# Edge stages of a graph-network kernel: ScalarE's loop announces its closing branch with a prefetch hint

## The chip, the core and the metric

The kernel runs on one NeuronCore of one Trainium2 chip. The metric is the device time of one execution in microseconds (us). Five engines run their own instruction streams and meet through semaphores: TensorE (PE, with its weight loads as PEld), VectorE (DVE), ScalarE (ACT), GpSimd (POOL) and the sync engine (SP), which issues DMAs.

## The reference, cut to what matters

The reference works on 6,250 nodes with 128 features and 100,000 edges sorted by destination. It chains two attention blocks over the graph. The first block has two GATv2 layers, and these are the edge stages that the change is about:

```python
def _gatv2(x, edge_index, Wl, bl, Wr, br, att, bias):
    ...
    xl = (x @ Wl + bl).reshape(n, h, d)
    xr = (x @ Wr + br).reshape(n, h, d)
    e = jax.nn.leaky_relu(xl[src] + xr[dst], NEG_SLOPE)
    score = jnp.einsum('ehd,hd->eh', e, att)
    m = jax.ops.segment_max(score, dst, num_segments=n)
    ex = jnp.exp(score - m[dst])
    denom = jax.ops.segment_sum(ex, dst, num_segments=n)
    alpha = ex / denom[dst]
    out = jax.ops.segment_sum(alpha[:, :, None] * xl[src], dst, num_segments=n)
    return out.reshape(n, h * d) + bias
...
x_in = _gatv2(x, edge_index, Wl1, bl1, Wr1, br1, att1, bc1)
h = jax.nn.relu(_batchnorm(x_in @ W1 + b1, g1, be1))
h2 = _gatv2(h, edge_index, Wl2, bl2, Wr2, br2, att2, bc2)
```

Each layer has three heads of 128 features. A third, different attention over the same edges (`edge_attention`) follows and is not touched.

## The kernel before

The kernel first sorts the edges, then runs GAT layer 1, a node layer, GAT layer 2, a second node layer, and the last attention. Both GAT layers call the same function, `gat_edges`, which is written once and so stands twice in every engine's program.

In `gat_edges` the edges and self loops are cut into 464 groups of 2 tiles of 128. Per group POOL gathers rows of the `xl` table into a ring in `feat_area` (L1332), PE looks up the destination's rows with one-hot matrices (L1382), DVE adds the two (L1524) and applies the leaky relu and the attention weights (L1532), and ScalarE sums each row over the features to a score (`reduce`, L1474: an ACTIVATE and an ACTIVATION_READ_ACCUMULATOR per tile and head, six pairs a group). Every eighth group closes a chunk: the scores are copied out (L1480), turned, scanned for the maximum of each destination and exponentiated (L1450, L1451). Eleven groups behind `reduce`, ScalarE multiplies the gathered rows by their weights (`weight`, L1458, four or six ACTIVATEs a group), and PE sums the weighted rows by destination (L1395) into `node_area`.

The order on each engine is written by `pipeline`. It takes stages with leads, writes the first groups out, then a loop whose turn holds `unroll` groups, then the last groups. In the edge stages `unroll` is 16. Each engine has its own loop with its own counter, so nothing joins the engines at the end of a turn but the semaphores of the stages. ScalarE's call is L1482. For it the loop runs over turns 2 to 28, which is 27 turns and 26 jumps back in each layer. Of ScalarE's program before, as it is built, a turn is 313 instructions of 64 bytes, the closing branch included. The loop's first instruction is number 1145 of that program in layer 1 and number 2110 in layer 2, counted from 0 without labels.

In the text below "loop 1" and "loop 2" are ScalarE's loops of `gat_edges` in layers 1 and 2, and a "turn" is one pass through such a loop. Operations that belong to the loop itself (counter, branch, the registers set at its head) have line L125.

Of the kernel before, what the change touches and what calls it, by code (L numbers as in the profile page):

```python
# [84 lines left out]
def later(g, n=1):  # L85

    return not isinstance(g, int) or g >= n
# [7 lines left out]
def snapped(eng, value):  # L95

    return value if isinstance(value, int) else eng.snap(value)


def pipeline(eng, groups, stages, unroll=2, number=False):  # L100

    ahead, behind = max(lead for lead, _ in stages), min(lead for lead, _ in stages)

    def at(turn, s):
        numbers = {}
        for lead, fn in stages:  # L110
            q = s + lead
            if isinstance(turn, int) and not 0 <= unroll * turn + q < groups:
                continue
            if not number:
                fn(turn + q // unroll, q % unroll)
                continue
            if q not in numbers:
                numbers[q] = snapped(eng, unroll * turn + q)
            fn(turn + q // unroll, q % unroll, numbers[q])

    first = -(-(unroll - behind) // unroll)
    last = (groups - ahead) // unroll
    for t in range(-ahead, unroll * first):
        at(t // unroll, t % unroll)
    with eng.Fori(first, last) as i:  # L125
        for s in range(unroll):
            at(i, s)
    for t in range(unroll * last, groups - behind):
        at(t // unroll, t % unroll)
# [135 lines left out]
def sort_by_dst(k, io, beside):  # L265
# [196 lines left out]
    with nc.Block() as block:  # L462
        @block.sync
        def _(sp):
            def load_keys(j, s):
                if s % 2:
                    return
                h = R * j + s
                if reused(j):
                    sp.wait_ge(ohT_ready, h - R + 2)  # L470
                sp.dma_start(lo_bc[s // 2], k.lo_edge[ds(h * (HALF * P), 2 * HALF * P)].partition_broadcast(P)
                             ).then_inc(bc_ready[s // 2], 16)

            pipeline(sp, halves, [(0, load_keys)], R)
            beside.on_sync(sp)
            src_moves.store(sp, k.moved_s, beside.moved_i)
            sp.sem_inc(sorted_src, 1)
            norm_on_sync(sp)
            table_on_sync(sp)

        @block.scalar
        def _(act):
# [15 lines left out]
            def mark_earlier(j, s):  # L498
# [4 lines left out]
                nc.scalar.activation(earlier[s % 2], match[s % 2], ACT.Relu).then_inc(earlier_set, 1)  # L503

            pipeline(act, halves, [(1, round_table), (1, keep_rows), (1, mark_earlier)], R)
            dst_moves.on_scalar(act)
            beside.on_scalar(act, multiplied, halves)
# [6 lines left out]
        def _(pe):  # L514
# [42 lines left out]
            def count_earlier(j, s):  # L557
# [5 lines left out]
                last.then_inc(looked, 1)  # L563

            pipeline(pe, halves, [(1, flip_keys), (1, match_keys), (0, update), (0, look_up), (0, count_earlier)], R)
            dst_moves.on_tensor(pe)
            beside.on_tensor(pe, dst_moves)
# [707 lines left out]
def gat_edges(k, att, tag, late):  # L1275

    nc = k.nc
    groups, U = GROUPS, 2 * CG
# [16 lines left out]
    first = [cut(1) for _ in range(2)]  # L1295
# [22 lines left out]
    def chunk(j, s):  # L1318
        return 2 * j + s // CG

    with nc.Block() as block:
        @block.gpsimd
        def _(pool):
            for g in range(groups):
                s = g % U
                if g >= U:
                    pool.wait_ge(summed, g - U + 1)
                    pool.nop(nofuse=True)
                for u in range(GS):
                    at = s * W + u * HE  # L1330
                    rows = k.gather_col[:, g * GS + u:g * GS + u + 1]
                    pool.indirect_dma_start(ring[:, at:at + HE], None, k.xl,  # L1332
                                            bass.IndirectOffsetOnAxis(ap=rows, axis=0)).then_inc(gathered[s], 16)
                late.write(pool, (g + 1) * LATE_GAT // groups - g * LATE_GAT // groups)
# [105 lines left out]
        @block.scalar  # L1440
        def _(act):
            def exps(j, s):
                if s % CG != CG - 1:
                    return
                c = chunk(j, s)
                act.wait_ge(shifted, c + 1)
                act.wait_ge(dropped, c + 1)
                if later(c):
                    act.wait_ge(back, c)
                nc.scalar.activation(ex, shift, ACT.Exp)  # L1450
                nc.scalar.activation(fade, drop, ACT.Exp).then_inc(exped, 1)  # L1451

            def weight(j, s):
                act.wait_ge(weights, chunk(j, s) + 1)
                for u in range(GS):
                    for h in range(H - 1 if s % 4 == 0 else H):
                        row = ring4[:, s * GS + u, h, :]
                        last = nc.scalar.activation(row[:, 0:D], row[:, 0:D], ACT.Copy, scale=row[:, D:D + 1])  # L1458
                last.then_inc(weighted, 1)

            def reduce(j, s):
                g = U * j + s
                c = chunk(j, s)
                act.wait_ge(weighed, g + 1)
                if s % CG == 0:
                    if later(c, 2):
                        act.wait_ge(scored, c - 1)
                    else:
                        act.wait_ge(preset, 1)
                for u in range(GS):  # L1470
                    for h in range(H):
                        at = z[s % V][:, u * HE + h * DW:u * HE + (h + 1) * DW]
                        to = h * CROW + s % CG * GS + u
                        last = nc.scalar.activation(at, at, ACT.Copy, accum_out=score_in[s // CG][:, to:to + 1])  # L1474
                last.then_inc(reduced, 1)
                if s % CG == CG - 1:
                    act.wait_ge(reduced, g + 1)
                    if later(c, 2):
                        act.wait_ge(turned, c - 1)
                    nc.scalar.copy(score[s // CG], score_in[s // CG]).then_inc(scored, 1)  # L1480

            pipeline(act, groups, [(-3, exps), (-11, weight), (0, reduce)], U)  # L1482

        @block.vector
        def _(dve):
# [792 lines left out]
```

## Time and profile before

| what | value |
|---|---|
| time, median of 3 runs | 6345.56 us |
| lowest and highest of the 3 | 6339.74, 6350.01 us |
| the profiled execution's own time | 6317.56 us |
| its span in the trace, first to last instruction | 6315.4 us |
| ACT busy over the span | 4432.6 us, 70% |
| DVE busy over the span | 5297.8 us, 84% |

The profiled execution took 28 us less than the median of the timed runs. Busy shares over the whole span mix stages with different limits, so the profile has to be read loop by loop: which engine has hardly any idle time in the stretch, what ended its idle time, and what the same program text did in the other layer. "Idle before, releaser" tells what an instruction waited for. "issue" there means that the trace shows no semaphore or transfer that ended the wait. The queue q14 of the DMA list is of the kind "instruction": it brings engines their own program.

### The profile page before, as it was taken

How to read it: one execution, taken by the hardware profiler on the slowest of the kernel's cores; microseconds unless marked ns; L12 is line 12 of the kernel's file. 1: busy time of each engine (PE TensorE's matmuls, PEld its weight loads, DVE VectorE, ACT ScalarE, POOL GpSimd, SP SyncE). 2: the span in 40 equal slices, each digit the busy share in tenths (PEclk: the TensorE clock that was granted, in tenths of full speed). 3: DMA queues.
4: the chain of work that ended last, by engine and by line, in shares of the span. 5: the costliest groups of instructions: out<-in, count | busy, mean ns of one | idle time of the engine just before them, and what ended most of it. 6: DMA issues, size and time to landing. Idle time of an engine off the chain costs nothing. (4 is left out here: it accounts for less than half of the span.)

```text
span 6315.4 us, 122309 instructions
## 1 busy us (share of the span) xinstructions
PE 4846.5 (77%) x22358; PEld 2873.2 (45%) x22359; DVE 5297.8 (84%) x12463; ACT 4432.6 (70%) x19858; POOL 4274.3 (68%) x3722
## 2 busy tenths in 40 slices
PE   3799689558988888888788888888888766666563
PEld 2575345234444444444644444444444445555552
DVE  9998898659999999999678898988888766666666
ACT  6487679429999999999278888888888553333332
POOL 0488777837777777776576676666666557777773
PEclk9999999779999999999899999999999977777776
DMA  0243000235555555556154444544445234444444
GB/s 16 54 86 30 2 2 2 31 116 144 140 139 140 137 141 139 140 139 114 27 152 130 125 129 127 131 124 127 129 125 124 42 106 130 128 129 128 129 129 77
DMA packets 342152, 657.19 MB, mean 104 GB/s; under 512 B 99030, under 2 KB 190100, under 8 KB 341506
## 3 DMA queue, kind: packets, MB, share of 16 engines
q0 software_dynamic: 191520, 481.83, 30.7%
q1 hardware_dynamic: 150370, 172.99, 10.7%
q14 instruction: 234, 1.92, 0.1%
q8 instruction: 28, 0.46, 0.0%
HBM read 618.58 MB, written 34.84 MB: 103 GB/s over the span
## 5 line engine op out<-in xcount | busy, mean ns | idle before, releaser
L1332 POOL DMA_INDIRECT feat_area<-xl_table,gather_col x1856 | 2178.9, 1174 | 948.3 <-issue 531.1
L1382 PE MATMUL bank<-node_area,feat_area 128*128 x3712 | 1481.2, 523 | 331.9 <-DVE feat_area L1524 146.2
L1458 ACT ACTIVATE feat_area<-feat_area 128x128 f32<-128x128 f32 x5104 | 1608.6, 419 | 145.8 <-issue 145.8
L1474 ACT ACTIVATE feat_area<-feat_area 128x130 f32<-128x130 f32 x5568 | 1500.4, 331 | 256.2 <-DVE feat_area L1532 254.4
L1395 PE MATMUL bank<-feat_area 128*128 128x390 f32 x3712 | 1433.4, 509 | 138.6 <-ACT feat_area L1458 90.2
L1382 PEld LDWEIGHTS bank<-node_area,feat_area 128*128 128x128 f32 x3712 | 646.9, 193 | 954.1 <-issue 701.7
L1474 ACT ACTIVATION_READ_ACCUMULATOR feat_area<-feat_area 128x1 f32 x5568 | 1054.3, 190 | 0.0
L1395 PEld LDWEIGHTS bank<-feat_area 128*128 128x128 f32 x3712 | 694.6, 195 | 694.8 <-issue 293.8
L2020 POOL DMA_INDIRECT feat_area<-kv_table,gather_src x832 | 808.1, 971 | 280.6 <-issue 252.1
L1524 DVE TENSOR_TENSOR feat_area<-bank,feat_area 128x780 f32<-128x780 f32 x928 | 890.0, 959 | 62.4 <-DMA feat_area<-xl_table,gather_col 43.8
L650 POOL DMA_INDIRECT word_by_dst<-feat_area,gather_col x640 | 791.8, 1237 | 195.0 <-issue 188.9
L1532 DVE SCALAR_TENSOR_TENSOR feat_area<-feat_area 128x780 f32<-128x780 f32 x928 | 889.8, 959 | 0.0
L2060 PE MATMUL bank<-feat_area 128*128 128x136 f32 x1664 | 362.1, 382 | 424.5 <-DVE feat_area L2131 423.7
L675 POOL DMA_INDIRECT word_by_src<-lo_src,gather_src x336 | 441.5, 1314 | 301.3 <-issue 146.4
L2073 ACT ACTIVATE feat_area<-feat_area 128x32 f32<-128x32 f32 x208 | 47.7, 229 | 734.5 <-DVE feat_area L2120 734.5
L2060 PEld LDWEIGHTS bank<-feat_area 128*128 128x128 f32 x1664 | 306.0, 267 | 473.6 <-DVE node_area L2146 326.7
L1571 DVE SCALAR_TENSOR_TENSOR node_area<-node_area,stays,bank 128x390 f32 x812 | 496.8, 612 | 15.5 <-PE bank L1395 15.3
L901 PE MATMUL bank<-feat_area 125*128 125x416 f16 (+1 forms) x2496 | 460.5, 347 | 7.9 <-ACT feat_area L917 4.8
L917 ACT ACTIVATE feat_area<-feat_area 125x128 f16<-125x128 f16 x1248 | 399.2, 390 | 75.2 <-DVE feat_area L875 64.2
L2107 DVE TENSOR_TENSOR feat_area<-feat_area,bank 128x512 f32<-128x512 f32 x208 | 143.1, 688 | 288.8 <-DMA feat_area<-kv_table,gather_src 284.2
L1063 DVE TENSOR_TENSOR feat_area<-iota_f,lo_col 128x256 f32<-128x256 f32 x928 | 384.6, 414 | 0.0
L901 PEld LDWEIGHTS bank<-feat_area 125*128 125x128 f16 x2496 | 243.6, 98 | 224.8 <-DVE feat_area L877 9.2
(363 smaller groups left out, 7140.4 us busy)
## 6 DMA issues: line engine op xcount, KB each, us to landing
feat_area<-lo_slot SPq DMA_DIRECT2D x464, 128.0 KB, 3.3
feat_area<-xl_table,gather_col POOLq DMA_INDIRECT x1856, 3.5
feat_area<-lo_slot_src SPq DMA_DIRECT2D x104, 256.0 KB, 3.4
node_area<-lo_edge SPq DMA_DIRECT2D x100, 256.0 KB
xl_table<-feat_area SPq DMA_DIRECT2D x98, 195.0 KB, 2.2
feat_area<-kv_table,gather_src POOLq DMA_INDIRECT x832, 2.8
feat_area<-gates SPq DMA_DIRECT2D x348, 32.0 KB
feat_area<-rowgates SPq DMA_DIRECT2D x696, 0.1 KB
```

What stands on the lines that cost most here:

```text
L650: pool.indirect_dma_start(k.word_d, bass.IndirectOffsetOnAxis(ap=self.pos[:, c:c + 1], axis=0), self.pair[:, c, :], None).then_inc(self.wr ...
L901: last = nc.tensor.matmul(self.out[p][m], sh.to_lane[s][:, p * P:(p + 1) * P], sh.to_tile[s][:, m * half:(m + 1) * half], start=False, sto ...
L1332: pool.indirect_dma_start(ring[:, at:at + HE], None, k.xl, bass.IndirectOffsetOnAxis(ap=rows, axis=0)).then_inc(gathered[s], 16)
L1382: last = nc.tensor.matmul(pair[s % 2][:, u, 0:HE], pick[s // 2 % 2][:, c:c + P], k.node[:, ds(columns[0], HE)], start=True, stop=True)
L1395: last = nc.tensor.matmul(sums_in[s % 2], place[s % 2][:, u * P:(u + 1) * P], ring[:, at:at + HE], start=u == 0, stop=u == GS - 1)
L1458: last = nc.scalar.activation(row[:, 0:D], row[:, 0:D], ACT.Copy, scale=row[:, D:D + 1])
L1474: last = nc.scalar.activation(at, at, ACT.Copy, accum_out=score_in[s // CG][:, to:to + 1])
L1524: nc.vector.tensor_tensor(z[s % V].rearrange("p (u e) -> p u e", u=GS), pair[s % 2][:, :, 0:HE], ring[:, s * W:(s + 1) * W].rearrange("p ( ...
L1532: nc.vector.scalar_tensor_tensor(out=zu, in0=zu, scalar=0.0, in1=att_w.unsqueeze(1).to_broadcast([P, GS, HE]), op0=ALU.max, op1=ALU.mult). ...
L1571: last = nc.vector.scalar_tensor_tensor(out=k.node[:, ds(to, HE)], in0=spare, scalar=k.stays[:, ds(g, 1)], in1=sums_in[s % 2], op0=ALU.mul ...
L2020: pool.indirect_dma_start(kv[s][:, u * KV:(u + 1) * KV], None, k.kv, bass.IndirectOffsetOnAxis(ap=rows, axis=0)).then_inc(gathered[s], 16)
L2060: last = nc.tensor.matmul(total[s % 2][u], place[s % 2][:, u * P:(u + 1) * P], wv[s % 2][:, u * VW:(u + 1) * VW], start=True, stop=True)
```

## The change

`pipeline` gets two more arguments, `head` and `hint`. The loop is opened with the same call as before, one level down, so that they can be passed on. `head` is given by no caller. `hint` is given by ScalarE's call in `gat_edges` alone. With it, the loop marks its first place in every turn, and the closing compare-and-branch is tied to this mark: ScalarE executes a branch prefetch hint there that names the closing branch.

```diff
-def pipeline(eng, groups, stages, unroll=2, number=False):
+def pipeline(eng, groups, stages, unroll=2, number=False, head=None, hint=False):
...
-    with eng.Fori(first, last) as i:
+    with eng.bass.Fori(first, last, engines=(eng.engine,), head_slot=None if head is None else {eng.engine: head},
+                       hint_back_edge=hint) as i:
         for s in range(unroll):
             at(i, s)
...
-            pipeline(act, groups, [(-3, exps), (-11, weight), (0, reduce)], U)
+            pipeline(act, groups, [(-3, exps), (-11, weight), (0, reduce)], U, hint=True)
```

The programs of PE, DVE, POOL and SP keep every instruction (their rows are the same but for line numbers, which move by one). ScalarE's program has 3,088 entries before and 3,090 after: two hints, one at the head of each loop. The label of each of these two loop heads carries a mark that it did not have.

ScalarE at the head of loop 1, before. The row ISA sets the turn's registers; L1458 is `weight`:

```order
L1480 COPY feat_area<-bank 128x51
L125 UNCONDITIONAL_BRANCH
L125 ISA
L1458 ACTIVATE feat_area<-feat_area 128x128 x6
L1464 ISA
```

The same place in the changed kernel, where L1459 is `weight`, L1481 the copy:

```order
L1481 COPY feat_area<-bank 128x51
L125 UNCONDITIONAL_BRANCH
L125 BRANCH_PREFETCH_HINT
L125 ISA
L1459 ACTIVATE feat_area<-feat_area 128x128 x6
```

The hint is the first instruction of a turn, ahead of the registers; the same holds at loop 2. Everything behind loop 1's head in ScalarE's program, loop 2 included, stands one instruction later than before.

ScalarE at the end of a turn of loop 1, changed kernel:

```order
L1475 ACTIVATE feat_area,bank<-feat_area 128x130 x6
L1481 COPY feat_area<-bank 128x51
L125 REGISTER_ALU
L125 COMPARE_AND_BRANCH
L1459 ACTIVATE feat_area<-feat_area 128x128 x12
```

Nothing is added or moved here: the last group's sums, the copy of the scores, the counter and the branch stand as before.

## Rows read from the trace of the kernel before

**Rows 1.** The page: span, busy time of each engine, busy tenths of ScalarE, granted clock.

```profile
span 6315.4 us, 122309 instructions
...
PE 4846.5 (77%) x22358; PEld 2873.2 (45%) x22359; DVE 5297.8 (84%) x12463; ACT 4432.6 (70%) x19858; POOL 4274.3 (68%) x3722
...
ACT  6487679429999999999278888888888553333332
```

**Rows 2.** Busy time of each engine by stretch: 26 periods of loop 1, of loop 2.

```profile
core 0: us, PE busy (x) PEld busy (x) DVE busy (x) ACT busy (x) POOL busy (x), PEclk, DMA share, GB/s
1559.30:2985.30 1426.00, 1264.27 (x3733) 628.12 (x3732) 1384.58 (x2907) 1354.08 (x7437) 1065.13 (x883) 1.00 0.54 138
3375.50:4959.00 1583.50, 1321.71 (x3733) 653.89 (x3732) 1387.67 (x2908) 1358.09 (x7437) 1055.93 (x883) 0.95 0.48 125
```

**Rows 3.** Loop operations (L125), loop 1: count, ns min/median/max, first and last start.

```profile
L125 ACTq COMPARE_BRANCH  x27: 40/45/50, 1559.3 to 2985.3; - x27
...
L125 PEldq COMPARE_BRANCH  x26: 76/208/212, 1555.2 to 2924.7; - x26
...
L125 ACTq FUSED_REGOPS  x26: 59/59/64, 1559.6 to 2929.8; - x26
```

**Rows 4.** The same for ScalarE in loop 2.

```profile
L125 ACTq COMPARE_BRANCH  x27: 40/45/45, 3375.5 to 4959.0; - x27
```

**Rows 5.** ScalarE's waits in loop 1: waiting line, releaser: us in total, times, longest.

```profile
ACT feat_area L1474 <- DVE feat_area L1532: 64.0, 93, 1.5
ACT feat_area L1458 <- issue: 5.5, 26, 0.2
```

**Rows 6.** ScalarE's waits in loop 2.

```profile
ACT feat_area L1458 <- issue: 140.3, 52, 5.5
ACT feat_area L1474 <- DVE feat_area L1532: 79.4, 86, 2.1
ACT feat_area L1450 <- DVE feat_area L1635: 3.6, 20, 0.2
```

**Rows 7.** Timeline of ScalarE at a turn's end in loop 1: start, us, what.

```profile
1722.06 0.20 ACT L1480 COPY feat_area<-bank 128x51 f32<-128x51 f32 x1
1722.47 0.99 ACT L1458 ACTIVATE feat_area<-feat_area 128x128 f32<-128x128 f32 x3 [0.21 <-issue]
```

**Rows 8.** Timeline of ScalarE in loop 2: first, a middle and last of 26 turn ends.

```profile
3378.04 0.40 ACT L1458 ACTIVATE feat_area<-feat_area 128x128 f32<-128x128 f32 x1 [2.41 <-issue]
3381.10 1.28 ACT L1458 ACTIVATE feat_area<-feat_area 128x128 f32<-128x128 f32 x4 [2.65 <-issue]
...
3497.36 0.20 ACT L1480 COPY feat_area<-bank 128x51 f32<-128x51 f32 x1
3500.00 0.40 ACT L1458 ACTIVATE feat_area<-feat_area 128x128 f32<-128x128 f32 x1 [2.44 <-issue]
3503.68 1.57 ACT L1458 ACTIVATE feat_area<-feat_area 128x128 f32<-128x128 f32 x5 [3.28 <-issue]
...
4898.01 0.40 ACT L1458 ACTIVATE feat_area<-feat_area 128x128 f32<-128x128 f32 x1 [5.46 <-issue]
4902.99 1.57 ACT L1458 ACTIVATE feat_area<-feat_area 128x128 f32<-128x128 f32 x5 [4.58 <-issue]
```

**Rows 9.** DMA queues in the 26 periods of loop 1: packets, MB, share.

```profile
q14 instruction: 12, 0.10, 0.0%
```

**Rows 10.** DMA queues in the 26 periods of loop 2.

```profile
q14 instruction: 142, 1.16, 0.3%
```

**Rows 11.** DMA queues behind one branch of loop 2, 3498 to 3506 us.

```profile
q14 instruction: 3, 0.02, 1.1%
```

**Rows 12.** Waits of all engines in loop 2, behind ScalarE's.

```profile
POOL feat_area L1332 <- PE bank L1395: 265.4, 190, 12.5
...
DVE feat_area L1615 <- PE bank L1425: 139.9, 26, 9.7
PE bank L1395 <- ACT feat_area L1458: 89.4, 20, 9.0
```

## The prediction

> **What bounds the kernel now.** I read the page first, then the two loops that the hint goes into, side by side. On the page ScalarE is busy 70% of the span, but its tenths stand at 9 through layer 1's edge stage and at 8 through layer 2's [rows 1]. Both stages run the same text over the same edges, so the reader is to ask what costs layer 2 a tenth. Next comes the view by stretch [rows 2]. The start times of ScalarE's closing branches give the stretches: 27 branches from 1559.3 to 2985.3 us in loop 1 and 27 from 3375.5 to 4959.0 us in loop 2, so 26 periods each [rows 3, 4]. Loop 1 takes 1426.0 us, 54.8 a period. Loop 2 takes 1583.5 us, 60.9 a period. ScalarE is busy 1354.1 and 1358.1 us in them: the same work, at 95% and at 86% of the time. In loop 1 ScalarE and VectorE (1384.6 us, 97%) are both close to full, so what one of them loses the stage loses.
>
> The waits tell where loop 2 loses it. In loop 1 the first ACTIVATE of a turn waits 26 times for "issue", 5.5 us in all [rows 5]. In loop 2 the same line waits 52 times for "issue", 140.3 us in all [rows 6]: two stalls a turn. The timelines show them. In loop 1 the branch costs a gap of 0.21 us [rows 7]. In loop 2 the gap is 2.44 us, then exactly one ACTIVATE runs, then comes a second gap of 3.28 us [rows 8]. Taken over all 26 turns, of which the group shows the first, a middle one and the last, the first gaps sum to 71.0 us (2.73 each) and the second to 69.3 us (2.67 each), together the 140.3 of the waits.
>
> The queue that brings instructions explains them. It moves 12 packets in loop 1 and 142 in loop 2 [rows 9, 10], 130 more, which is 5 a turn. Three of a turn's packets fall into the 8 us from a turn's branch on [rows 11]. A packet is 1.16 MB / 142 = 8.2 kB, so 128 instructions of 64 bytes. ScalarE's program thus comes in blocks of 128 instructions. In loop 2 a turn fetches again what it had; in loop 1 it does not.
>
> Where the heads stand tells why. In loop 2 two instructions run between the two gaps, the registers (L125) and one ACTIVATE, so the head is 2 instructions short of a block's end: slot 126. Loop 1's head is 2110 - 1145 = 965 instructions earlier, 7 blocks and 69, so at slot 57. The turn has 313 instructions. Loop 1 ends at 57 + 313 = 370, inside its third block (384). Loop 2 ends at 126 + 313 = 439, in a fourth. Three blocks are kept from turn to turn, four are not.
>
> **What the change does, part by part.** (1) It adds one hint a turn, 54 in all. (2) It moves loop 2's head. One added instruction in loop 1 moves it from slot 126 to 127. Loop 2's own hint is then the only instruction left in that block. Whether the head stays at 127 decides the result. If the added hints take one slot more between them, or if the marked label is put at a block's start because it falls one short of it, loop 2's turn begins at slot 0 or just behind it, and with 314 instructions it ends at 314, in its third block, as loop 1's does. (3) The hint itself may let the block of the loop's head be fetched before the branch jumps there.
>
> The price of (1): the trace has no hint. It stands at the head of a turn, where ScalarE is idle and its queue is empty (the copy of the scores waits for the last sum, and the gap is 0.21 us [rows 7]), so nothing hides it. The nearest rows are the registers set at the same place, 59 ns, ScalarE's branch, 45 ns, and at the far end TensorE's branch, 208 ns [rows 3]. A hint that overlaps the 0.21 us gap costs 0, and no row gives a reason for a gain. I take 59 ns, the row of the same place: 54 x 0.059 = 3.2 us. The ends are 0 and 54 x 0.208 = 11.2 us.
>
> The price of (2): if loop 2 behaves as loop 1, ScalarE's idle time in it falls from 1583.5 - 1358.1 = 225.4 us to loop 1's 1426.0 - 1354.1 = 71.9 us, so 153.5 us go. As bounds, the two gaps alone less what loop 1 keeps give 140.3 - 5.5 = 134.8 us, and the difference of the two stretches gives 157.5 us. The 18.7 us between 134.8 and 153.5 are ScalarE's waits for VectorE, 79.4 against 64.0, and for the shift of the scores, 3.6 against none [rows 5, 6]: they follow from the stalls, since VectorE waits in turn for sums that ScalarE's weighting holds up, PE 89.4 us at L1395 for ScalarE, VectorE 139.9 us at L1615 for a transpose that stands behind these sums in PE's queue [rows 12]. What comes late next is what loop 1 shows: VectorE's L1532 for 64.0 us. No other engine stands in the way. In loop 2 VectorE is busy 1387.7, PE 1321.7 and POOL 1055.9 us, all under the 1426 to 1430 us that would remain, and PE's granted clock, 0.95 here, was 1.00 in loop 1 with fewer holes [rows 2].
>
> The price of (3) without (2): the first gap of a turn goes and the second stays, because the block behind the head is needed after a single instruction whether or not the head's block was there. That is 71.0 - 5.5 = 65.5 us.
>
> The sum for (1) and (2), against the profiled execution: 6317.6 - 153.5 + 3.2 = 6167.3 us. The timed runs have a median 28 us above that execution. The stalls are not known there, so I take the same difference off the median: 6345.6 - 150.3 = **6195 us**. Should all of the 28 us lie in these stalls, the time is 6345.6 - 181.5 = 6164 us. With the small end of the gain and the large end of the hint it is 6345.6 - 134.8 + 11.2 = 6222 us.
>
> **A rule of the Trainium skill beside this.** Runtime: NRT & Kernel Launch, section "Instruction fetch mechanics", states that an engine other than TensorE keeps two blocks of 256 instructions, that fetching ahead is purely sequential, and that a taken branch out of these two has to wait for its block. The last of it agrees with the 2.44 us gap. The block's size does not: the packets here are 8.2 kB, so 128 instructions, and there are 5 of them a turn. By the page's two blocks of 256, a head at a block's start would give the same 6195 us.
>
> **The rivals.** *The hint alone works.* The head stays at slot 127 and only the jump's own gap goes: 6345.6 - 65.5 + 3.2 = 6283 us. For it speaks that one hint is one row in the order and 126 + 1 is 127. Against it speaks that the label was marked, and that one slot more is enough.
>
> *Nothing changes.* The hint is executed in the head's block while this block is present, so it has nothing to fetch, and four more fetches push the block out before the branch comes; the head stays at 127. Then 6345.6 + 3.2 = 6349 us, 0.05% more. For it speaks that of the 5 packets a turn 3 come where one turn ends and the next begins [rows 11] and so 2 in mid-turn, after the hint and before the branch. The Trainium skill's page named above has the rule for it, fetching ahead being purely sequential, and by that rule the time is this one unless the head moves.
>
> *It gets slower.* The hint brings the head's block again though it is present, and that copy takes the place of a block that the turn still needs. Loop 1, which fetches nothing now [rows 9], would then fetch like loop 2 and lose what loop 2 loses, 153.5 us, while loop 2 stays: 6345.6 + 153.5 + 3.2 = 6502 us. It decides from the point at which a turn's blocks and the hinted copy are more than are kept; loop 1 keeps three at least and loop 2 shows that four a turn are too many. Against it speaks that loop 1's 26 jumps bring no packet at all for blocks that are present: the 12 packets are there in both loops (142 less 130) and belong to programs that are written out, as POOL's is (883 gathers and writes in each stretch) [rows 2].
>
> **How the numbers follow.** Head at a block's start and all stalls gone: 0.70, 6195 us, with 6164 to 6222 as its own range. The hint alone: 0.14, 6283 us, up to 6345.6 - 65.5 + 11.2 = 6291. Nothing: 0.08, 6349 us. Slower: 0.08, 6502 us. A measurement of this kernel tells changes over about 0.2%, 12.7 us, from none. Faster is 0.70 + 0.14 = 0.84, within 0.2% is 0.08, slower is 0.08. The range reaches over the first two cases, 6164 to 6291 us; with the spread beyond each one's own bounds it holds about 8 in 10.
>
> **What would show each step.** Right: ScalarE's closing branches in loop 2 come every 55.0 us and not every 60.9; its L1459 waits for "issue" about 5.5 + 26 x 0.06 = 7 us in each loop, 0.27 us a turn; the instruction queue has about 12 packets in loop 2; VectorE is busy over 95% of it; the hint's own row says x54 and about 60 ns. The hint alone: one gap of 2.7 us a turn, still with fetches, and a period near 58.3 us. Nothing: 52 gaps and 142 packets. Slower: gaps and packets in loop 1. What would make the prediction wrong: a head that stays short of a block's end, a hint that costs over 0.2 us, or a loop 2 that without its stalls is held by something else than loop 1 is.

## The result and the profile after

The changed kernel takes 6183.56 us (median of 4 runs, 6181.87 to 6184.52) where the kernel before takes 6345.5 us (median of 4). The ratio is 0.9745 with a 95% interval of 0.9728 to 0.9762, so 2.5% faster. 6195 us was forecast, with a range of 6164 to 6291.

The page of the changed kernel, beside [rows 1]: span, busy times, ScalarE's busy tenths, and the queue of instructions over the whole span, which read 234 packets and 1.92 MB before.

```profile
span 6179.7 us, 122363 instructions
...
PE 4796.4 (78%) x22358; PEld 2847.2 (46%) x22359; DVE 5312.0 (86%) x12463; ACT 4427.3 (72%) x19858; POOL 4289.9 (69%) x3722
...
ACT  6477679637999999999539999999999553333332
...
q14 instruction: 104, 0.85, 0.1%
```

ScalarE's tenths now stand at 9 in layer 2's edge stage too. The span fell by 135.7 us and the queue by 130 packets. Loop 2 alone gives more, 150.2 us (below); the profiled execution of after was 13 us later at loop 1's first closing branch (1572.3 against 1559.3), where a single hint was all that the change had added so far.

The two loops after, beside [rows 2], the same columns: busy time of each engine, granted clock, DMA. Each stretch runs from the first closing branch to the last, 26 periods.

```profile
1572.30:2998.50 1426.20, 1264.28 (x3733) 628.28 (x3732) 1384.68 (x2907) 1352.24 (x7437) 1067.95 (x883) 1.00 0.55 138
3388.40:4821.70 1433.30, 1265.86 (x3733) 629.82 (x3732) 1386.23 (x2907) 1353.69 (x7437) 1061.44 (x883) 1.00 0.55 138
```

Loop 1 is what it was (1426.2 against 1426.0 us). Loop 2 takes 1433.3 us where it took 1583.5, so 150.2 us went there, and VectorE is busy for 97% of it. ScalarE's waits in loop 2, beside [rows 6] (the change adds one line ahead, so L1459 is the weighting and L1475 the sums):

```profile
ACT feat_area L1475 <- DVE feat_area L1533: 70.8, 106, 1.5
ACT feat_area L1459 <- issue: 6.3, 26, 0.3
```

The 52 gaps and 140.3 us of "issue" are 26 gaps and 6.3 us, one a turn at the branch, as in loop 1. The end of one turn in loop 2, beside [rows 8]:

```profile
4047.82 0.20 ACT L1481 COPY feat_area<-bank 128x51 f32<-128x51 f32 x1
4048.27 1.57 ACT L1459 ACTIVATE feat_area<-feat_area 128x128 f32<-128x128 f32 x5 [0.24 <-issue]
```

The loop's own operations in loop 2, beside [rows 4]: the branch, the hint and the registers with count and ns.

```profile
L125 ACTq COMPARE_BRANCH  x27: 44/49/59, 3388.4 to 4821.7; - x27
L125 ACTq BRANCH_PREFETCH_HINT  x26: 31/31/31, 3388.6 to 4765.7; - x26
L125 ACTq FUSED_REGOPS  x26: 59/59/65, 3388.7 to 4765.7; - x26
```

The instruction queue in loop 2's 26 periods, beside [rows 10]: 12 packets where there were 142.

```profile
q14 instruction: 12, 0.10, 0.0%
```

The result alone does not tell what did it. Two causes fit: the head of loop 2 came to a block's start, so that a turn ends in its third block (theory P, with M for "the marked label is moved there"), or the hint fetched or kept what the loop needed (theory H; S is the case that the head stays short of the block's end). The experiments separate them.

### The profile page after: what moved, and what is told of

It is laid out like the page before. It is cut to its first block and busy times, and to the rows that moved or that the text cites. A ratio compares the mean times of both kernels' runs of the same rounds, so it can differ in the third digit from the quotient of the medians.

```text
span 6179.7 us, 122363 instructions
## 1 busy us (share of the span) xinstructions
PE 4796.4 (78%) x22358; PEld 2847.2 (46%) x22359; DVE 5312.0 (86%) x12463; ACT 4427.3 (72%) x19858; POOL 4289.9 (69%) x3722
## 3 DMA queue, kind: packets, MB, share of 16 engines
q1 hardware_dynamic: 150370, 172.99, 10.4%
## 5 line engine op out<-in xcount | busy, mean ns | idle before, releaser
L1383 PE MATMUL bank<-node_area,feat_area 128*128 x3712 | 1458.7, 516 | 355.7 <-DVE feat_area L1525 153.1
L1475 ACT ACTIVATE feat_area<-feat_area 128x130 f32<-128x130 f32 x5568 | 1498.0, 329 | 249.6 <-DVE feat_area L1533 247.3
L1459 ACT ACTIVATE feat_area<-feat_area 128x128 f32<-128x128 f32 x5104 | 1604.6, 418 | 13.1 <-issue 13.1
L1396 PE MATMUL bank<-feat_area 128*128 128x390 f32 x3712 | 1398.1, 499 | 18.9 <-issue 6.5
L1475 ACT ACTIVATION_READ_ACCUMULATOR feat_area<-feat_area 128x1 f32 x5568 | 1043.6, 188 | 0.0
L1396 PEld LDWEIGHTS bank<-feat_area 128*128 128x128 f32 x3712 | 681.8, 191 | 559.4 <-issue 143.7
L1533 DVE SCALAR_TENSOR_TENSOR feat_area<-feat_area 128x780 f32<-128x780 f32 x928 | 889.4, 958 | 0.0
L2061 PE MATMUL bank<-feat_area 128*128 128x136 f32 x1664 | 345.3, 369 | 425.8 <-DVE feat_area L2132 425.3
L2061 PEld LDWEIGHTS bank<-feat_area 128*128 128x128 f32 x1664 | 290.1, 254 | 476.8 <-DVE node_area L2147 326.8
L2051 PE MATMUL bank<-node_area,feat_area 128*128 x1664 | 338.9, 373 | 14.6 <-ACT feat_area L2087 9.9
```

Of the source, the lines that this page charges most:

```text
L1383: last = nc.tensor.matmul(pair[s % 2][:, u, 0:HE], pick[s // 2 % 2][:, c:c + P], k.node[:, ds(columns[0], HE)], start=True, stop=True)
L1396: last = nc.tensor.matmul(sums_in[s % 2], place[s % 2][:, u * P:(u + 1) * P], ring[:, at:at + HE], start=u == 0, stop=u == GS - 1)
L1533: nc.vector.scalar_tensor_tensor(out=zu, in0=zu, scalar=0.0, in1=att_w.unsqueeze(1).to_broadcast([P, GS, HE]), op0=ALU.max, op1=ALU.mult). ...
L2061: last = nc.tensor.matmul(total[s % 2][u], place[s % 2][:, u * P:(u + 1) * P], wv[s % 2][:, u * VW:(u + 1) * VW], start=True, stop=True)
```

## Experiments: the head's place

In the runs below, "packets" are those of the instruction queue and "issue" is ScalarE's idle time ahead of the weighting's line, both in one loop from its first closing branch to its last; where the head is placed by hand, from the branch into the loop, so 27 turns and the entry's 5 packets with them. All ratios are against the kernel before on the same chip. It took 6338.11 us beside the runs with the hint in one loop and those with one and two more instructions, 6332.48 us beside those at slots 71, 72 and 100, and 6331.39 us beside those with longer turns. The expected times start from the 6345 and 6183 us of the first pair, so a measured one may lie up to 14 us lower for that alone.

**The hint in loop 1 alone** (this moves loop 2's unmarked head by one slot):

```diff
-            pipeline(act, groups, [(-3, exps), (-11, weight), (0, reduce)], U, hint=True)
+            pipeline(act, groups, [(-3, exps), (-11, weight), (0, reduce)], U, hint=tag == 1)
```

> The hint in loop 1 alone; loop 2 has no hint and no marked label, and its head moves from slot 126 to 127. Theory P (only the place of loop 2's head counts: it pays where the 313 instructions end in a fourth block): 127 + 313 = 440 ends in the fourth block, so loop 2 keeps two gaps a turn, about 140 us for issue, 142 packets of instructions, and the time stays at 6345 to 6350 us. Theory H (the hint fetches ahead what the loop needs): loop 1 had nothing to gain and loop 2 has no hint, so the same 6345 to 6350 us. Both fall if loop 2's gaps go: then one instruction of shift was enough and neither the mark nor the second hint was needed. In either case loop 1 shows the hint's price alone: 31 ns a turn.

Measured: 6345.74 us, ratio 1.0009 (0.9999 to 1.0019). ScalarE's wait in loop 2:

```profile
ACT feat_area L1459 <- issue: 156.9, 26, 10.2
```

Its instruction queue:

```profile
q14 instruction: 142, 1.16, 0.3%
```

All of the gain is gone. Only the shape of the stalls changed: 26 longer ones instead of 52, since at slot 127 no ACTIVATE stands between the two fetches any more. That ACTIVATE took 0.40 us [rows 8] and ran between the gaps at slot 126; over 26 turns this is 10.4 us of the 16.6 by which 156.9 us here exceed the 140.3 before. Loop 1 shows the hint alone, 6.3 us of issue where it had 5.5, so 31 ns a turn.

**The hint in loop 2 alone** (`hint=tag == 2`; nothing is added ahead of it):

> The hint in loop 2 alone; nothing is added ahead of it, so its head would be at slot 126 as before. Theory P with a moved label (a marked label that falls just short of a block's end is put at the next block's start): all gaps of loop 2 go, about 12 packets, 6183 us. Theory P without a moved label: the head stays at slot 126, 126 + 314 = 440, a fourth block, 6345 us, if the hint itself does nothing. Theory H (the hint fetches the head's block ahead): one or both gaps go, 6280 us or 6185 us; if both go, the start of the turn shows whether the head was moved, since under H the packets stay at about 142 and under P they fall to about 12.

Measured: 6180.78 us, ratio 0.9749 (0.9733 to 0.9765), with 6.3 us of issue and 12 packets in loop 2. The whole gain is loop 2's hint. The run does not yet say by which of its two effects.

**No hint, one more instruction ahead of loop 2, and two more.** They are increments of an unused semaphore at the start of ScalarE's part of layer 1's edge stage. The edit is shown for one more, against the changed kernel; for two it has `range(2 ...)`:

```diff
+    spare_sem = k.sem(f"a{tag}_spare")
...
-            pipeline(act, groups, [(-3, exps), (-11, weight), (0, reduce)], U, hint=True)
+            for _ in range(1 if tag == 1 else 0):
+                act.sem_inc(spare_sem, 1)
+            pipeline(act, groups, [(-3, exps), (-11, weight), (0, reduce)], U)
```

> No hint. One semaphore increment on an unused semaphore is added at the start of ScalarE's program of layer 1's edge stage, so loop 2's head stands at slot 127 (and loop 1's at 58). Theory P: 127 + 313 = 440, a fourth block, two gaps a turn with no ACTIVATE between the second and the first but the registers alone: 6345 us, 142 packets. Theory H: 6345 us as well, there is no hint. A time near 6183 us would say that any shift by one cures loop 2.

> No hint. Two semaphore increments at the same place: loop 2's head stands at slot 128, a block's start, loop 1's at 59. Theory P: 313 instructions end in the third block, so all gaps of loop 2 go without any hint: 6182 us, about 12 packets, period 55 us. Theory H: without a hint nothing is gained: 6345 us, 142 packets.

Measured, one more: 6348.49 us, ratio 1.0018 (1.0008 to 1.0028), 150.8 us of issue and 142 packets in loop 2. One turn's end with one more (L1483 copy, L1461 weighting):

```profile
4060.61 0.20 ACT L1483 COPY feat_area<-bank 128x51 f32<-128x51 f32 x1
4066.87 0.40 ACT L1461 ACTIVATE feat_area<-feat_area 128x128 f32<-128x128 f32 x1 [6.07 <-issue]
```

Measured, two more: 6183.21 us, ratio 0.9753 (0.9736 to 0.9769). ScalarE's wait in loop 2 with two more:

```profile
ACT feat_area L1461 <- issue: 5.5, 26, 0.2
```

Its instruction queue:

```profile
q14 instruction: 12, 0.10, 0.0%
```

Two increments of a semaphore that nobody waits for do what the hint in loop 2 does on the same chip, 6183.21 against 6180.78 us. One gains nothing: it is 10 us slower than before, as the ACTIVATE that no longer runs between the fetches would have it. With no hint in these programs this is the place of the head and nothing else, and it confirms the slot worked out in the prediction: 126 before, 128, a block's start, with two more.

**No hint, both heads placed by hand at slot 71, and at slot 72** (`head=71`, `head=72` instead of `hint=True`):

> No hint, both heads at slot 71: 71 + 313 = 384, the last slot of the third block, so three blocks are just enough. Theory P: no gap but the branch's 0.21 us, about 12 packets a loop, 6182 us. If the real limit is lower (a block is fetched ahead of the last slots), gaps appear in both loops already here and the time is about 6313 us.

> No hint, both heads at slot 72: 72 + 313 = 385, so the closing branch alone stands in a fourth block. Theory P: one slot more than the run at 71 brings 5 packets a turn and the jump's gap in both loops, 65 us each: 6183 + 130 = 6313 us. If the count of blocks is not the cause, one slot changes nothing: 6182 us.

Measured at 71: 6170.6 us, ratio 0.9745 (0.9728 to 0.9762), 5.3 us of issue in loop 2 and 17 packets, the entry's included. Measured at 72: 6392.26 us, ratio 1.0098 (1.0078 to 1.0117). One slot costs 221.7 us. ScalarE's wait in loop 2 at 71:

```profile
ACT feat_area L1459 <- issue: 5.3, 26, 0.2
```

Its instruction queue:

```profile
q14 instruction: 17, 0.14, 0.0%
```

ScalarE's wait in loop 1 at slot 72:

```profile
ACT feat_area L1459 <- issue: 106.6, 27, 6.5
```

The same in loop 2 at slot 72:

```profile
ACT feat_area L1459 <- issue: 108.3, 26, 7.2
```

And the instruction queue at slot 72, the same row in both loops:

```profile
q14 instruction: 147, 1.20, 0.3%
```

71 + 313 = 384 is three blocks to the slot, and 385 is not. So the count of blocks of 128 instructions decides. The size at 72 was expected too small, 6313 us. One gap a turn appears as expected, but it is 4 us long and not 2.7:

```profile
4025.22 1.86 ACT L1459 ACTIVATE feat_area<-feat_area 128x128 f32<-128x128 f32 x6 [3.88 <-issue]
```

The trace's packets behind a branch say why. With the branch alone in the fourth block, two packets start between the branch and the next turn's first instruction at each of loop 2's 26 jumps (three at two of them): here 0.7 and 2.1 us behind the branch. The next turn starts 1.2 to 1.4 us after the last of them has landed. In the kernel before it is a single packet in all but one of the gaps, from 0.9 us on, and the turn starts about 1.0 us after it has landed. So at slot 72 the first packet is most likely the block behind the loop, asked for as the turn enters its fourth block, and the one that is needed stands behind it. The trace doesn't name the block of a packet; this is read from order and times.

## Experiments: what the hint itself does

**Both heads at slot 100, without and with the hint.** A turn ends at 100 + 313 = 413, in a fourth block, and the head stands 28 slots short of its block's end. Whether it stays there is looked at below.

```diff
-            pipeline(act, groups, [(-3, exps), (-11, weight), (0, reduce)], U, hint=True)
+            pipeline(act, groups, [(-3, exps), (-11, weight), (0, reduce)], U, head=100)
```

> No hint; the heads of both loops are placed at slot 100 of a block, so each turn ends at 100 + 313 = 413, in the fourth block, and 28 instructions stand between the head and the block's end. Theory P: both loops now fetch 5 blocks a turn, 260 more packets than the changed kernel's 104 in all. The jump's gap is there in both loops, 2.7 us less 0.2, 65 us each. The second gap should be small, since the 28 instructions take about 4 us of ScalarE and a block comes in 2.5 to 3 us: 6183 + 130 = 6313 us; with the second gap in full, 6183 + 270 = 6453 us. Theory H says the same, there is no hint.

> The same places, slot 100, with the hint in both loops: here the hint has something to fetch and the label is not moved. Theory P alone (the hint does nothing but stand there): as the run without the hint, 2 us more. Theory H (the hint brings the head's block before the branch): the jump's gap falls to 0.24 us in both loops while packets stay at about 5 a turn, and the time is near 6185 us, so about 130 us below the run without it.

Measured without the hint: 6275.1 us, ratio 0.9902 (0.9881 to 0.9923). With it: 6177.01 us, ratio 0.9756 (0.9739 to 0.9773). ScalarE's wait in loop 2, without the hint:

```profile
ACT feat_area L1459 <- issue: 73.1, 26, 5.3
```

Its instruction queue:

```profile
q14 instruction: 148, 1.21, 0.3%
```

ScalarE's wait in loop 2, with the hint:

```profile
ACT feat_area L1459 <- issue: 6.7, 27, 0.3
```

Its instruction queue:

```profile
q14 instruction: 17, 0.14, 0.0%
```

Two things were expected and came: the second gap is gone where 28 instructions stand ahead of the block's end, and the hint takes the first one. One was not expected by either theory: with the hint there are no packets. The hint does not fetch the head's block early here, it makes fetching needless, and four blocks are then kept from turn to turn.

Was this marked head left at slot 100? Had it been put at a block's start, three blocks would have done and the missing packets would say nothing of the hint. The first turn of loop 1 settles it. A packet starts as the turn enters its second block and its third: 5.0 and 26.8 us behind the branch into the loop without the hint, 5.0 and 26.3 us with it. (From slot 71 these are 8.0 and 31.0 us.) So the head stands at the same slot with and without the hint. The next entry differs. Without the hint a packet starts at 49.9 us, as the turn enters its fourth block:

```profile
q14 instruction: 1, 0.01, 0.7%
```

This is the queue from 1564.5 to 1570 us; with the hint the same stretch has no packet of it. So the hint at the head keeps the entry of the last block from fetching one more. In later turns without the hint such a packet comes again, in most 5 to 6 us ahead of the next branch. It is most likely the block behind the loop, and that it pushes out the head's is inferred from the fetch that follows the next branch; the trace names no blocks.

The size without the hint was expected as 6313 us and is lower. Loop 2's period is 57.0 us against 54.9 at slot 71, 2.1 us for a gap that is 2.5 us longer: part of the gap is time that ScalarE would otherwise have waited for VectorE, and these waits are 61.2 us against 70.9 at slot 71.

**Was the head of the changed kernel moved?** Both effects cure loop 2, so neither the result nor the run with loop 2's hint alone can tell. They part where a turn is longer. 96 increments of unused semaphores a turn, in loop 2 alone, make it 410 instructions with the hint. Two further runs have the same and `head=111` or `head=96` for loop 2:

```diff
+    spare_sems = [k.sem(f"a{tag}_spare{n}") for n in range(6)]
...
             def reduce(j, s):
...
+                if tag == 2 and not isinstance(j, int):
+                    for spare_sem in spare_sems:
+                        act.sem_inc(spare_sem, 1)
```

From slot 127 such a turn needs five blocks, from a block's start four.

> As the changed kernel, but a turn of loop 2 holds 96 more instructions (increments of unused semaphores, six a group), so 410 with the hint. The head's natural slot is 127 as in the changed kernel. Theory M (a marked label just short of a block's end is put at the block's start): 0 + 410 ends in the fourth block, the hinted loop of four blocks fetches nothing, as the run at slot 100 with the hint did: about 12 packets in loop 2 and gaps of 0.24 us. Theory S (the head stays at 127, and the changed kernel's loop 2 was cured by the hint alone over four blocks): 127 + 410 = 537 ends in a fifth block, packets and gaps as in the run at slot 111. The fillers may cost up to 96 x 27 x 0.035 = 90 us where nothing hides them, so packets and gaps decide, not the time.

> The same fillers and the hint, but loop 2's head is placed at slot 111: 111 + 410 = 521, a fifth block for sure. It tells what five blocks with a hint look like. If the hint fetches the head's block ahead, packets come every turn (4 or more, 110 to 140 in loop 2) but the jump's gap stays at 0.24 us; a second gap may appear 17 instructions behind the head. If the hint only keeps four blocks from being pushed out, there is also the jump's gap of 2.7 us.

> The same fillers and the hint with loop 2's head at slot 96: 96 + 410 = 506, four blocks. The control for the fillers: about 12 packets, gaps of 0.24 us, and the time that the fillers cost, 6183 us to 6270 us. The run with the natural head should equal it under theory M.

Measured: 6173.28 us with the natural head (ratio 0.9753, 0.9737 to 0.9769), 6187.5 us at slot 111 (0.9773, 0.9757 to 0.979) and 6173.09 us at slot 96 (0.9752, 0.9735 to 0.9768). ScalarE's wait in loop 2 with the natural head:

```profile
ACT feat_area L1461 <- issue: 6.3, 26, 0.3
```

Its instruction queue:

```profile
q14 instruction: 11, 0.09, 0.0%
```

ScalarE's waits in loop 2 with the head at slot 111, five blocks for sure (L1480 is the sums' line here, the second gap):

```profile
ACT feat_area L1480 <- issue: 19.1, 25, 2.6
ACT feat_area L1461 <- issue: 15.3, 27, 2.6
```

Its instruction queue:

```profile
q14 instruction: 150, 1.23, 0.3%
```

ScalarE's wait in loop 2 with the head at slot 96, four blocks (2.8 of the 9.3 us are the jump into the loop):

```profile
ACT feat_area L1461 <- issue: 9.3, 27, 2.8
```

Its instruction queue:

```profile
q14 instruction: 18, 0.15, 0.0%
```

The natural head behaves as four blocks and not as five. So the head was not left at slot 127: 410 instructions end in a fourth block only from slot 102 or below. Where it stands the entry into the loop tells. A MOVE of line L125 is the last instruction that the trace shows ahead of the head. With one more instruction and no hint, head at slot 127, the head's first instruction starts 0.07 us behind it:

```profile
L125 ACTq MOVE  x1: 35/35/35, 3332.0 to 3332.0; - x1
L125 ACTq FUSED_REGOPS  x1: 65/65/65, 3332.1 to 3332.1; - x1
```

With two more, where the head is the first instruction of a block, it takes 0.35 us:

```profile
L125 ACTq MOVE  x1: 35/35/35, 3340.0 to 3340.0; - x1
L125 ACTq FUSED_REGOPS  x1: 65/65/65, 3340.3 to 3340.3; - x1
```

And in the changed kernel, 0.39 us:

```profile
L125 ACTq MOVE  x1: 35/35/35, 3333.6 to 3333.6; - x1
L125 ACTq BRANCH_PREFETCH_HINT  x1: 31/31/31, 3333.9 to 3333.9; - x1
```

In loop 1 of the changed kernel, whose head lies inside a block, the hint starts 0.07 us behind the MOVE, so the hint itself isn't the 0.3 us. The run with the longer turn has 0.40 us and the one with the hint in loop 2 alone 0.43 us. In all three the marked head of loop 2 stands at a block's start, also where its natural slot was 126.

The fillers cost nothing that can be measured (ratio 0.9753, as with two more instructions and no fillers), and ScalarE's waits show no issue gap besides the 26 at the branch.

**Five blocks without the hint** (as at slot 111, loop 2's hint left out):

> As the run at slot 111, without loop 2's hint: 111 + 409 = 520, five blocks. Packets 5 to 6 a turn, the jump's gap of 2.7 us and a second one behind the 17 instructions left in the head's block, at most 1.5 us. Against the hinted run at slot 111 it shows what a hint is worth where a turn's blocks cannot all be kept: 65 us if it removes the jump's gap, about none if it only protects four blocks.

Measured: 6250.15 us, ratio 0.9872 (0.9856 to 0.9889). ScalarE's waits in loop 2:

```profile
ACT feat_area L1461 <- issue: 77.6, 27, 4.9
ACT feat_area L1480 <- issue: 28.9, 27, 2.7
```

Its instruction queue:

```profile
q14 instruction: 176, 1.44, 0.3%
```

Against the hinted run this is 62.6 us more, the 65 us expected for a hint that removes the jump's gap. Both wait rows fall with the hint, 77.6 to 15.3 and 28.9 to 19.1 us. The packets fit one reading of all runs: off the 17 or 18 that a loop without refetching shows, 176 leaves 6 a turn and 150 leaves 5. Without a hint a turn of five blocks brings its five and the one behind the loop, with a hint the head's comes in the place of the one behind. The starts bear this out: with the hint a packet starts 1 to 2 us ahead of nearly every branch, as the turn enters its fifth block, and at the 26 jumps back none lies between the branch and the next turn's first instruction, which follows after 0.4 to 0.6 us (once 0.9); without the hint one lies there in every turn. So here the hint does bring the head's block early.

## Why the prediction was right

- **What bounds the kernel.** It held that loop 2 would take loop 1's time once its stalls were gone. 1433.3 us against 1430 worked out; what is late next is VectorE's L1533, for which ScalarE waits 70.8 us, as it said, and PE's granted clock is 1.00 there where it was 0.95.
- **The slots.** 57 and 126, three blocks against four. The runs at 71 and 72, and those with one and two more instructions, show both the limit (384) and loop 2's slot to the instruction. "Four are not kept" holds without a hint only: with one, four are.
- **The hint's own price.** 59 ns were taken and it took 31 ns, both in its row and in the gap, 0.24 against 0.21 us. 54 x 0.031 = 1.7 us against 3.2.
- **The gain.** 153.5 us were taken and 150.2 us are seen in the profiled loop. The medians differ by 162, inside the 181.5 that was the far end. (That end took the hint as free; with its 3.2 us it is 178.3.) The profiled execution of before was 28 us below its median, and that of after 2 us below (6181.87 us). The prediction left open whether these 28 us lie in the stalls. Where the 12 us between 150.2 and 162 lie no trace shows. Some may be stalls: with the head at slot 127 two profiled executions differ by 6 us in them (150.8 and 156.9). The time came out 11 us below the 6195 forecast.
- **The head at a block's start, given 0.70.** This was the case, and the longer turn and the entry into the loop show it. In part this was luck: that a marked label is moved was an assumption, since no row spoke for it.
- **"The hint alone", 6283 us.** This rival's price was wrong. It held that the second gap stays, as the block behind the head would still have to come. The run at slot 100 shows that with four blocks the hint leaves nothing to fetch. Had the head stayed at 127, the turn would have had four blocks and the hint would most likely have given the same time; that was not run. So the measured time alone doesn't speak for the moved head, and the prediction's number was safer than its 0.70 said.
- **"Nothing changes"** and **"slower"** fell. The hint acts though it is executed while the head's block is present (slot 100), and in loop 1, where all is present, 12 packets stay 12.

The Trainium skill's page Runtime: NRT & Kernel Launch, section "Instruction fetch mechanics", holds that fetching ahead is purely sequential. Without a hint the runs agree, as far as packets tell: a turn of four blocks brings five, the last as it enters its fourth block. With a hint they do not: 17 packets in place of 148 at slot 100, and none as the fourth block is entered.

## What to carry to other kernels

Count the instructions of an engine's loop and look where its head stands. All of this was measured on ScalarE alone. If the profile has "issue" gaps of 2 to 4 us at the first instruction of a turn and instruction packets that grow with the turns, the turn needs one block more than is kept, and an edit anywhere ahead of the loop on that engine can switch this on or off. A slower or faster time after a harmless edit may be only that. Compare the same loop at its other copy first, as here layer 1 with layer 2. Then place the head, shorten the turn, or hint the branch; the hint is the safest of the three, since it costs 31 ns a turn, also worked with four blocks, and was not a loss where nothing was to be gained (loop 1). But it also moves what stands behind it: loop 1's hint alone put loop 2's head from slot 126 to 127, and a head at slot 71 would by the same step come to slot 72, the dearest one here.

## What the runs showed of the hardware

- ScalarE's program came in packets of 8.2 kB, 128 instructions. Three blocks in a turn were kept without a hint (0 refetches at 313 instructions from slot 71), four with one (0 refetches at 410 instructions from slot 96), and five were not (5 packets a turn with the hint, 6 without).
- One slot too many costs 4.1 us a turn: 221.7 us over 54 turns, between slots 71 and 72. It is dearer than being 29 slots over: 104.5 us, between 71 and 100. A turn that spills by only its branch has the worst place that was tried without a short head block.
- With a short head block two fetches follow each other: 5.4 us a turn at slot 126 and 5.8 to 6.0 at 127, measured in loop 2 as idle time at the branch and just behind it.
- A marked loop head whose natural slot was 127 or 126 stood at the next block's start: 0.39 to 0.43 us from the MOVE ahead of the loop to the head, 0.35 us for an unmarked head at a block's start, 0.07 us for heads inside a block.
- With the hint at slot 100 no packet starts as the turn enters its fourth block; without it one does, 49.9 us into the first turn.
